# A graph layer on one core: edges are filed in pairs of node tiles, and the count of filed edges is taken over partitions first

## The reference

```python
xn = layernorm(x)
# graph convolution, twice: (h = xn, W of 256x512, relu; then W of 512x256)
agg = segment_sum(h[src] and h[dst], other end) / max(degree, 1)
h   = h @ W0 + b0 + agg @ W1 + b1
# linear attention over all nodes, 8 heads
p   = k.T @ v / N ; mix = (q @ p) @ Wfc.T + bfc
x   = x + h + mix
# 8 experts, top 2, 256 -> 512 -> 256, relu
x   = x + combine(experts(layernorm(x)))
```

## Time and profile before

| | us |
|---|---|
| median of 3 runs | 2232.6 (2228.12 to 2233.89) |
| the profiled execution | 2227.12 |
| its span | 2225.2 |
| PE busy | 2067.5 (93% of the span) |
| DVE busy | 1544.1 (69%) |
| ACT busy | 1210.1 (54%) |

### The profile page before, as it was taken

One profiled execution on the slowest core, in us unless ns is written; L12 is line 12 of the kernel. 1 busy time (PEld: TensorE's weight loads), 2 busy tenths in 40 slices (PEclk: granted clock), 3 DMA queues, 4 the chain that ended last, 5 costly groups with the idle time before them and its releaser, 6 DMA issues.

```text
span 2225.2 us, 52275 instructions
## 1 busy us (share of the span) xinstructions
PE 2067.5 (93%) x15356; PEld 1305.8 (59%) x15357; DVE 1544.1 (69%) x4838; ACT 1210.1 (54%) x2515; POOL 367.8 (17%) x434
## 2 busy tenths in 40 slices
PE   3888889999999999999999998999999995999996
PEld 2676675555555555555554543444444443899996
DVE  6998977999999999998555544455444544455554
ACT  4777754555555555555656543444444443666664
POOL 2000000000000000000111111111222112466665
PEclk9999998999999999999999999999999997999998
DMA  3333246222222222223444336555555555555552
GB/s 95 93 95 92 89 126 190 113 109 116 116 117 116 109 117 116 112 112 128 167 144 147 119 120 219 199 198 197 193 194 194 195 212 177 129 94 93 88 94 42
DMA packets 158734, 299.11 MB, mean 134 GB/s; under 512 B 31774, under 2 KB 107855, under 8 KB 156419
## 3 DMA queue, kind: packets, MB, share of 16 engines
q1 hardware_dynamic: 131075, 243.66, 31.6%
q0 software_dynamic: 25856, 47.15, 9.4%
q10 hardware_dynamic: 1664, 6.35, 0.8%
HBM read 148.32 MB, written 144.19 MB: 131 GB/s over the span
## 4 chain that ended last, share of the span: by engine, by line
PE 68%; issue 13%; DVE 9%; DVEq 4%; DMA 2%; POOL 1%; ACT 1%; POOLq 1%; ACTq 0%; SPq 0%
PE bank L2280 44%; PE bank L2271 6%; PE bank L2519 6%; PE bank L2504 6%; DVE big L1132 1%; DVE big L1145 1%; DVE big L1127 1%; PE bank L2486 1%; DVEq L1141 1%; PE bank L2288 1%; POOLq L843 1%; DVE big L1143 1%; DMA rows_dram<-big 1%; DVEq L1129 1%; DMA big<-rows_dram 1%
## 5 line engine op out<-in xcount | busy, mean ns | idle before, releaser
L2280 PE MATMUL bank<-RW,big 128*128 128x512 f16 x4753 | 1148.3, 380 | 0.0
L2280 PEld LDWEIGHTS bank<-RW,big 128*128 128x128 f16 x4753 | 431.3, 98 | 384.5 <-issue 3.2
L1929 ACT ACTIVATE big<-bank 128x512 f16<-128x512 f32 (+1 forms) x640 | 364.2, 573 | 316.1 <-PE bank L2271 316.1
L1301 DVE TENSOR_TENSOR big<-iotaB,keys 128x512 f16<-128x512 f16 x1300 | 452.4, 420 | 8.0 <-issue 6.8
L2271 PEld LDWEIGHTS bank<-big 128*128 128x128 f16 x2560 | 190.8, 98 | 106.3 <-DVE big L1301 1.5
L2271 PE MATMUL bank<-big 128*128 128x128 f16 x2560 | 247.2, 219 | 0.8 <-DVE big L1301 0.8
L986 POOL DMA_INDIRECT out_dram<-big x112 | 179.8, 1605 | 109.9 <-ACT big L2074 75.5
L910 POOL DMA_DIRECT2D big<-in_L_ffn_W_dram x8 | 6.2, 777 | 1041.3 <-DVE R L1360 1040.6
L2065 ACT ACTIVATE big<-bank,b1A,iscA 128x256 f32<-128x256 f32 x224 | 114.0, 559 | 99.0 <-PE bank L2504 88.5
L2504 PE MATMUL bank<-big,RW 128*128 128x256 f16 x1344 | 157.3, 274 | 0.4 <-ACT big L2054 0.4
L2519 PE MATMUL bank<-RW,big 128*128 (+1 forms) x1344 | 156.9, 274 | 0.2 <-DVE big L1724 0.2
(11 more groups left out here) (422 smaller groups left out, 2919.2 us busy)
## 6 DMA issues: line engine op xcount, KB each, us to landing
big<-a_dram SPq DMA_DIRECT2D x48, 800.0 KB, 6.0
big<-a_dram SPq DMA_DIRECT2D x48, 768.0 KB, 4.2
a_dram<-big SPq DMA_DIRECT2D x49, 640.0 KB, 3.0
a_dram<-big SPq DMA_DIRECT2D x49, 512.0 KB, 2.6
a_dram<-big SPq DMA_DIRECT2D x49, 416.0 KB, 2.4
big<-rows_dram SPq DMA_DIRECT2D x56, 265.0 KB
big<-in_x_dram SPq DMA_DIRECT2D x96, 128.0 KB, 2.1
own_dram<-big SPq DMA_DIRECT2D x48, 256.0 KB, 2.5
```

The costliest lines, as they stand in the source:

```text
L1301: last = v.tensor_tensor(out[q].rearrange("p b (m k) -> p b m k", k=2), inturn(iotaB[:, :], QB, P // 2), twice(kd[:, q * QB:(q + 1) * QB, ...
L1929: a.activation(Ab[q][:, 0:n], banks[BB(q)][:, 0:n], ACT.Copy).then_inc(s_ab, 1)
L2280: last = mm(bank[:, :], blk(q, c), R2[:, u * 2 * D:(u + 1) * 2 * D], start=(i == 0), stop=(i == T - 1))
```

## The change

The filing stage goes in pairs p of tiles (2p and 2p + 1; PAIRS = 25). OH, V, R1, base, held and rank2 hold two tiles each; V and R1 have two buffers instead of three and two, the second of each in R3. `onehots`, `ranks` and `inverse` take a pair in one instruction per operation; V becomes a step of its own (`values`) after `inverse`. The product with base is written over OH. ACT and PE keep their instructions per tile and handle two tiles of `base1`, `table1`, `before1` and `file1` at a time. The count of filed edges is summed by PE over partitions first (five matmuls over `cover`), then by DVE along the row; `fit` multiplies the keys of each tile as they are copied, in place of TT and TU, and `digits` reads those copies.

Some extra steps move to other tiles of the loop. DVE: `words1`, `keys1`, `same1`, `within1` come at t % 7 = 0, 1, 2, 3 (before: 2, 3, 4, 5), `decode` stays at t % 7 = 1, `scales1` goes from t = 30 to 34, L1251 from 34 to 38. ACT: L1855 comes at t = 12, 14, 16 (before 11, 13, 15), L1874 at 31 (29), L1878 at 36 (32), L1883 at 41 and 43 (36, 38); the squares (L1865) stay at t = 17 to 24. In the diff, the first hunks are DVE's, then ACT's, then PE's.

```diff
+            def pair(p):
+                n = min(2, T - 2 * p) * CAP
+                return n, slice(2 * p * CAP, 2 * p * CAP + n)
+            def onehots(p):
+                n, sl = pair(p)
+                if p >= 2:
+                    dve.wait_ge(s_before, 2 * p - 2)
+                v.tensor_tensor(OH[p % 2][:, 0:n * U].rearrange("p (c m k) -> p c m k", c=n, k=2),
+                                inturn(iotaU[:, :], n, U // 2), twice(key2[:, sl, :], n, U // 2),
                                 ALU.is_equal).then_inc(s_oh, 1)
                 dve.drain()
+            def values(p):
+                n, sl = pair(p)
+                if p >= 2:
+                    dve.wait_ge(s_filed, 2 * p - 2)
+                v.tensor_tensor(V[p % 2][:, 0:n * U].rearrange("p (c m k) -> p c m k", c=n, k=2),
+                                OH[p % 2][:, 0:n * U].rearrange("p (c m k) -> p c m k", c=n, k=2),
+                                twice(ends[:, sl, :], n, U // 2), ALU.mult).then_inc(s_val, 1)
+                dve.drain()
+            def ranks(p):
...
+                dve.wait_ge(s_base, 2 * p + a)
...
-            def inverse(t):
-                i = t % 2
-                dve.wait_ge(s_std, t + 1)
-                if t >= 2:
-                    dve.wait_ge(s_xn, t - 1)
-                v.reciprocal(rstd[:, i:i + 1], sums[:, i, 3:4]).then_inc(s_stat, 1)
+            def inverse(p):
+                n = min(2, T - 2 * p)
+                dve.wait_ge(s_std, 2 * p + n)
+                if p:
+                    dve.wait_ge(s_xn, 2 * p)
+                v.reciprocal(rstd[:, 0:n], sums[:, 0:n, 3]).then_inc(s_stat, n)
...
+            onehots(0)
+            values(0)
+            for p in range(PAIRS):
+                if p + 1 < PAIRS:
+                    onehots(p + 1)
+                ranks(p)
+                if p + 1 < PAIRS:
+                    inverse(p + 1)
+                    values(p + 1)
+                for t in range(2 * p, min(2 * p + 2, T)):
...
-            v.tensor_scalar(cover, TT[:, 0:T * TC], 0.5, None, ALU.is_ge)
+            v.tensor_scalar(cover, TT[:, 0:T * TC], 0.5, None, ALU.is_ge).then_inc(s_flag, 1)
+            dve.wait_ge(s_fp, 2)
+            v.tensor_reduce(small[:, 56:57], banks[4][:, :], AX.X, ALU.add)
             dve.drain()
-            v.tensor_reduce(small[:, 56:57], cover, AX.X, ALU.add).then_inc(s_flag, 1)
-            dve.wait_ge(s_fp, 2)
-            v.tensor_scalar(fit[:, :], banks[4][:, 0:1], float(2 * EDGES), None, ALU.is_equal)
...
-            v.tensor_scalar(TT[:, 0:T * TC], TT[:, 0:T * TC], fit[:, 0:1], None, ALU.mult)
-            v.tensor_scalar(TU[:, 0:T * TC], TU[:, 0:T * TC], fit[:, 0:1], None, ALU.mult).then_inc(s_flag, 1)
+            v.tensor_scalar(fit[:, :], small[:, 56:57], float(2 * EDGES), None, ALU.is_equal)
+            v.tensor_scalar(flag[:, :], small[:, 56:57], float(2 * EDGES), None, ALU.not_equal).then_inc(s_flag, 1)
...
-                        v.tensor_scalar(kd[:, :, :], deep(tab[:, bass.ds(col, TC)], [P, TC, 2]), 1.0, None, ALU.mult)
+                        v.tensor_scalar(kd[:, :, :], deep(tab[:, bass.ds(col, TC)], [P, TC, 2]),
+                                        fit[:, 0:1], None, ALU.mult)
...
             base1(0)
+            base1(1)
             for t in range(T):
                 normal1(t)
-                if t + 1 < T:
-                    base1(t + 1)
-                if t:
-                    table1(t - 1)
+                if t % 2 == 0:
+                    for i in range(t + 2, min(t + 4, T)):
+                        base1(i)
+                    for i in range(max(t - 2, 0), t):
+                        table1(i)
                 if t >= 3:
                     own1(t - 3)
                 if t + 2 < T:
                     deviation1(t + 2)
                 place1(t)
                 low1(t)
...
             before1(0, 0)
+            before1(1, 1)
             for t in range(T):
-                if t + 1 < T:
-                    before1(t + 1, (t + 1) % 2)
+                if t % 2 == 0:
+                    for i in range(t + 2, min(t + 4, T)):
+                        before1(i, i % 2)
                 gram(t)
                 if t >= 2:
                     own1(t - 2)
-                file1(t, t % 2)
+                if t % 2 or t == T - 1:
+                    for i in range(t // 2 * 2, t + 1):
+                        file1(i, i % 2)
...
             pe.wait_ge(s_flag, 1)
-            mm(banks[4][:, 0:1], ones[:, :], small[:, 56:57], start=True, stop=True).then_inc(s_fp, 1)
+            for c in range(0, T * TC, 4 * P):
+                n = min(4 * P, T * TC - c)
+                last = mm(banks[4][:, 0:n], ones16, cover[:, c:c + n], start=(c == 0), stop=(c + 4 * P >= T * TC))
+            last.then_inc(s_fp, 1)
```

More of the change, by code:

```diff
@@ L1148, in ranks @@
                 dve.drain()
[L1149 to L1152, removed]
+                if p >= 2:
+                    dve.wait_ge(s_filed, 2 * p - 2)
+                v.tensor_tensor(R1[p % 2][:, 0:n * DEPTH].rearrange("p (c m k) -> p c m k", c=n, k=2),
+                                inturn(iotaR[:, 0:DEPTH], n, DEPTH // 2), twice(rank2[:, 0:n, :], n, DEPTH // 2),
@@ L1219, in _ @@
             within1(0)
-            onehots(0, 0)
-            for t in range(T):
-                g, i = t // PACK + 1, t % PACK
-                if t + 1 < T:
-                    onehots(t + 1, (t + 1) % 2)
-                ranks(t, t % 2)
-                if t + 1 < T:
[L1227 to L1252, removed]
-                    last.then_inc(s_wpl, 1)
@@ new lines, in _ @@
+            onehots(0)
[8 more added lines that the diff above has]
+                for t in range(2 * p, min(2 * p + 2, T)):
+                    g, i = t // PACK + 1, t % PACK
+                    if g < NG:
+                        if i == 0:
+                            words1(g)
+                        if i == 1:
+                            keys1(g)
+                        if i == 2:
+                            same1(g)
+                        if i == 3:
+                            within1(g)
+                    if i == 1 and t > PACK:
+                        decode(t // PACK - 1)
+                    if t == 12:
+                        dve.wait_ge(s_w, 16 * 16)
+                        v.tensor_tensor(bhs[:, :], bh[:, 0, :], bh[:, 1, :], ALU.add).then_inc(s_bh, 1)
+                    if t == 28:
+                        dve.wait_ge(s_sp, 1)
+                        v.tensor_reduce(small[:, 35:39], banks[4][:, 0:8].rearrange("p (a k) -> p a k", k=2), AX.X, ALU.add)
+                        v.tensor_copy(small[:, 39:40], banks[4][:, 8:9]).then_inc(s_sp, 1)
+                    if t == 34:
+                        scales1()
+                    if t == 38:
+                        dve.wait_ge(s_wph, 1)
+                        for k in range(2):
+                            last = v.scalar_tensor_tensor(out=W1T[1][:, k, :], in0=W1s[:, k, :], scalar=wsc,
+                                                          in1=W1T[0][:, k, :], op0=ALU.mult, op1=ALU.subtract)
+                        last.then_inc(s_wpl, 1)
@@ L2112, in before1 @@
                 for c in range(CAP):
-                    last = mm(banks[par][:, 0:U], lower, OH[par][:, c * U:(c + 1) * U], start=(c == 0), stop=(c == CAP - 1))
+                    last = mm(banks[par][:, 0:U], lower, OH[t // 2 % 2][:, (par * CAP + c) * U:(par * CAP + c + 1) * U], start=(c == 0), stop=(c == CAP - 1))
                 last.then_inc(s_before, 1)
             def file1(t, par):
-                pe.wait_ge(s_val, t + 1)
-                pe.wait_ge(s_rank, t + 1)
+                pe.wait_ge(s_val, t // 2 + 1)
+                pe.wait_ge(s_rank, t // 2 + 1)
                 if t >= 2:
@@ L2122, in file1 @@
                 for c in range(CAP):
[L2123 to L2124 removed]
+                    last = mm(banks[2 + par][0:DEPTH, 0:U], R1[t // 2 % 2][:, (par * CAP + c) * DEPTH:(par * CAP + c + 1) * DEPTH],
+                              V[t // 2 % 2][:, (par * CAP + c) * U:(par * CAP + c + 1) * U], start=(c == 0), stop=(c == CAP - 1))
                 last.then_inc(s_filed, 1)
```

73 lines of the change are left out of this document (30 added, 43 removed).

## The result

The changed kernel took 2303.9 us (median of 4 runs, 2299.4 to 2309.0), the kernel before 2233.0 (4 runs): ratio 1.032, 95% interval 1.030 to 1.035, slower. The forecast was 2292 us, with 2265 to 2316 as its range. The profiled execution after took 2302.7 us with a span of 2301.1, and the one before a span of 2225.2, so the two traces differ by 75.9 us.

The account below looks back on a forecast made before the run. DVE was taken to bound filing, PE the aggregation. Loop 41.5, start 3.4, first keys 3, ACT's steps 5.4, clock 8.7, stage end 3 and count 0.5 sum to 65.5 us on 2227.1: 2292 us, range 2265 to 2316.

Parts of the forecast that it names:

- The loop: Filing stage: inverse to next inverse closes through DVE, PE and two ACT steps; 11.06 us per pair against 9.06, +41.5 us.
- three links: Parts of the filing loop per plain pair: DVE 2.59 us, PE 1.21, ACT's two steps 4.73 + 2.53.
- Extra steps: Filing stage: DVE's keys, decode and scales lie in the loop and stay exposed at their old price of 59.5 us.
- first keys: Early filing stage: words1(1), moved from t = 2 to t = 0, waits for its last window transfer; +3 us.
- ACT's own steps: Filing stage: ACT's squares, evacuations and scalings at even t lie inside the loop, 9 x 0.60 us; +5.4 us.
- clock: Filing stage: PE idles ahead of before1, its clock falls, two before1 run slower in 13 pairs; +8.7 us.
- Start: Start of filing: inverse(0) waits for two deviations, and the first onehots and values are twice as long; +3.4 us.
- End of the stage: End of filing: ACT's wait for the own_dram store behind the last, padded load falls into the loop; +3 us.
- count: Count of filed edges: five PE matmuls and a short reduction come, two multiplications go; +0.5 us.
- `fit` as a factor: Aggregation's keys copy: costs nothing per tile, as DVE has 8% to spare; without that cover 0.1 us, 5 in all.
- the aggregation unchanged: One of the signs named for the changed profile: the aggregation behind the filing stage stays as it was.
- DVE keeps the pace: Rival, filing stage: the loop has slack and the shorter DVE work shows; 2209 or 2199 us, chance 0.06.

Follow-up runs that it names:

- the first remedy: Changed kernel with ACT's two base1 copies of the next pair moved to the odd step behind deviation1; 2293.1 us, ratio 1.028.
- e5: Changed kernel with PE's before1 of tile t+2 behind gram of tile t, and ACT's base1 behind deviation1 or normal1; 2244.2 us, ratio 1.005.
- e2: Changed kernel with DVE's keys1, same1, within1, decode and scales issued between ranks and inverse, ahead of its wait; 2247.4 us, ratio 1.008.
- e4: Kernel before with one edit: the keys copy multiplies by the flag's column in memory, not by constant 1.0; 2238.3 us, ratio 1.0026.
- e10: Kernel before with the second of a tile's two keys copies left out; 2229.9 us, ratio 0.9992.
- e6: Changed kernel with e5's orders, the kernel before's count and keys copy, and words1 to within1 at their old steps; 2230.5 us, ratio 0.9997.
- e8: e6 with PE's own1 ahead of before1 in even steps and DVE's same1, within1, decode, scales before inverse; 2227.9 us, ratio 0.9985.
- e11: e8 with 309 small memsets added at DVE's start, giving the aggregation's loop the kernel before's instruction numbers; 2224.8 us, ratio 0.9961.

## Why the prediction was right, and where it was off

*The loop: right.* Its three links were forecast as 2.59 + 1.21 + 7.26 us. Measured at the pair shown: 87.56 - 84.97 = 2.59, 88.76 - 87.56 = 1.20, 95.91 - 88.76 = 7.15, together 10.94 for 11.06. At that length 23 rounds come to 38.7 us more than before, for 41.5. `ranks` was to take 5.3; it takes 92.92 - 87.60 = 5.32. ACT's first wait was forecast as 1.4 us, and was 1.49. What I had not seen is the second path through `gram`. It changed no number, but it made the first remedy fail. e5 bears the loop out. The Trainium skill's rule on grouping (page "Perfetto Trace Analysis", section "Optimizing Scalar/DVE Operations") doesn't decide this case: the 91% of the earlier trace rows met the condition of its first half, and the changed kernel, with DVE at 68% and PE waiting 64.0 us for it, that of its second. But e5 got the time back with the larger instructions, by the orders alone, so the loop has to be looked at first.

*Extra steps, first keys, ACT's own steps, clock: right in kind, a little small.* The rest of the 59.9 us is 21.2 for a forecast of 3 + 5.4 + 8.7 = 17.1. Of these the window's wait was 5.47 us, 4.6 more than the 0.89 before; forecast 3. Two slow `before1`, 1.83 us for 1.16, came in 13 of the 23 rounds, as counted, for 0.67 each. That leaves 7.9 us for ACT's own steps, forecast 5.4, and for all else; a square on ACT took about 1 us, where I had put 0.60, because the accumulator's read (0.19 us) and its gaps go with it. That the old extra steps stay exposed was right as well: e2, which moves them ahead of the wait, wins 52.8 us in the stage.

*Start: right.* 38.30 - 34.65 = 3.65 for 3.4.

*End of the stage and count: not separable, and met in part by luck.* 3 + 0.5 were forecast, and the stretch up to the first `build` grew by 4.0. ACT waited 2.06 us for `own_dram` there, and the five matmuls took 2.31 us at a granted clock of 0.50, for 2.4. But the stretch itself varies by 5 us among the runs. In e2, with the clock at 1.00 there, it is 3.6 us shorter than in the changed kernel, though ACT waited longer for the store there, 2.52 us. So the forecast's 3 us for the store aren't shown.

*`fit` as a factor: wrong, the one step that failed.* The prediction said that it "costs nothing per tile", since "DVE has 8% to spare beside PE", and priced the case without that cover at 0.1 us per tile, 5 in all. That was the case: 0.11 us per tile, 5.4 in all. With it failed the sign "the aggregation unchanged": 680.6 us became 686.1. The 8% were gaps between instructions, not time in which DVE could have done more. The earlier trace rows can't tell the two apart; the timeline of one tile, where no gap ends with another engine, gave the hint, and e4 shows it. DVE was already the later of the two engines, by 0.03 us a tile (e10).

*Against the median.* 2292 is 12 us under the measured 2303.9. The factor makes 5.4 of it. The sum started from an execution that was 5.5 us below the median, which I had written down but not added back. The rest is the small terms, of which the loop came out 2.8 us shorter than forecast and most others longer.

The rival "DVE keeps the pace" was put at 2199 to 2209. Its condition was that ACT passes `base1` before it needs `onehots`; in e5 it does, and still the merged instructions give less than priced: the last `onehots` comes 8.0 us earlier than before in e6, and 11.5 in e8.

## What to carry to other kernels

Before two tiles are put into one instruction, write down the order in which each queue reaches the steps of a round, and follow what each needs: a loop that closes within one round is paid with its whole length, and it must be opened on every queue that it passes (in the stage, opening it on ACT alone gave 7 us here, with `before1` on PE 56). Steps that stand in front of a wait on their engine are hidden by it as far as it lasts, and the same steps behind it are paid (53 us of the stage here, without one instruction less). Count an engine as having room only if its timeline shows waits that end with another engine; DVE, 92% busy with nothing but issue gaps, was full here.

## What the runs showed of the hardware that was not expected

DVE's gap ahead of one instruction of a loop can be 0.10 us longer or not, by where the loop lies in DVE's program: 0.26 against 0.15 us ahead of `oneA`, or 0.31 against 0.21 ahead of the keys, in each of 14 tiles, with the same instructions in the same order. Here that is 5 us of the run. At the place that the loop had in the kernel before, the gap is gone (e11). In both cases the 0.10 us lie in DVE's sequencer, between the end of a drain and the start of the next instruction: 0.13 us where the kernel before has 0.03, although the histogram that `oneA` waits for was done 4 us earlier. Which places bring it, and why, stays open; three places were tried with these keys. The kernels with the factor (730, 1039 and 1042 instructions ahead) show neither gap, so their 0.11 us a tile is the copy's.

A TENSOR_SCALAR of 128x104 f16 takes 0.27 us with its factor in a column of memory and 0.21 with a constant; from the start of one to the start of the next it is 0.19 and 0.13.
